# Attention kernel: the exponential of a pair of heads in two parts, with two sums

## The chip, the cores and the metric

The kernel runs on one core of a Trainium2 chip. The time is the device time of one execution in microseconds. The engines work side by side, each through its own list of instructions in order, and wait for each other through semaphores: TensorE (PE) does matrix products and transposes, VectorE (DVE) and ScalarE (ACT) work on tiles element by element, GpSimd (POOL) does slower side work, and SyncE (SP) issues the transfers.

## The reference

A block of a perceiver in float32: 32 batches of 64 queries, each against a context of 1601 keys of 256 features, in 16 heads of 16 features. After the cross-attention come a feed-forward part with cosines and a mixture of experts; the change touches only the attention. Its core is

```python
q = _split_heads(query @ Wq.T + bq)
k = _split_heads(key @ Wk.T + bk)
v = _split_heads(value @ Wv.T + bv)
score = jnp.einsum('bhqd,bhkd->bhqk', q, k) * SCALE
attn = jax.nn.softmax(score, axis=-1)
out = jnp.einsum('bhqk,bhkd->bhqd', attn, v)
out = out.transpose(0, 2, 1, 3).reshape(query.shape[0], query.shape[1], D)
return out @ Wp.T + bp
```

## The kernel before

The function `cross_attention` works through the 32 batches, and in each through 8 *pairs* of heads. One pair is a tile of 128 rows (two heads of 64 queries) by 1601 keys. The time in which TensorE takes one pair's scores is called a *slot* here, slots 0 to 7 in a batch. The running number of a pair is `g`, its number in the batch `p`.

What TensorE does in slot p, in its order (lines 643 to 695):

1. `scores(b, p)`, L587: four products into the four score banks `ps_s`. It waits until VectorE has read the scores of the pair before (`max_ready`).
2. Transposes 0 to 7 of the pair *before*, `turn(.., 0)` and `turn(.., 1)`, L598: each `turn` turns up to four blocks of 128 keys of `probs` into one of the two banks of `ps_t` (bank i % 2). They wait for the probabilities (`probs_ready`) and for their bank: `turn 0` for the copy that emptied bank 0 of the pair before that one (L595), `turn 1` for VectorE's copy of the tail from bank 1.
3. A step of the next batch's keys or values (L550 to L552). Slot p has the steps in `SLOT_STEPS` (L36), one to three.
4. Transposes 8 to 12, `turn(.., 2)` and `turn(.., 3)`: they wait until ScalarE has copied bank 0 and bank 1 of `turn 0` and `turn 1`.
5. In slots 0 and 4, after the transposes, the turned scale (L605) and `weigh` (L618), the product of four pairs' probabilities with the values. In the other slots, the rest of the steps.

ScalarE (lines 395 to 414) copies banks of transposes from PSUM to SBUF (L380, three copies of 512 columns for each pair) and takes the exponential of a whole pair in place (L386), with the row sum into `esum` by the accumulator output. That output is an instruction of its own, ACTIVATION_READ_ACCUMULATOR. In slots 0 and 4 the order is copy 0, copy 1, copy 2, exponential; in all other slots it is copy 0, copy 1, exponential, copy 2.

VectorE takes the minimum over a pair's negated scores and moves them to `probs` (L424, `take_scores`), which releases the exponential, adds the bias to the keys' steps and splits them in two (L442, L444), copies the values (L449) and the tail of the transposes (L456). Twice in a batch, in slots 0 and 4, `spread_scale` takes the reciprocals of four pairs' sums (L466) and spreads them over a tile (L468), ahead of `take_scores`.

The last batch has no steps of a next one. The order on every engine is written out by hand; no planner is at work.

Of the kernel before, what the change touches and what calls it, by code (L numbers as in the profile page):

```python
# [8 lines left out]
ALU = mybir.AluOpType  # L9
ACT = mybir.ActivationFunctionType  # L10
AX = mybir.AxisListType

P = 128
B, SQ, D = 32, 64, 256
SK = 1601
H, HD = 16, 16
NC = D // P
PAIRS = H // 2
# [19 lines left out]
HALF = PAIRS // NC  # L38
# [178 lines left out]
def cross_attention(nc, ctxT, x, q_scr, wk, bk, wv, bv, wp, rows, ident, x1_scr, x1_mv):  # L217
    with ExitStack() as ctx:
        sb = lambda n, s, d=F32: ctx.enter_context(nc.sbuf_tensor(n, s, d))
# [7 lines left out]
        probs = sb("a_probs", [P, 2, SKP])  # L227
# [9 lines left out]
        own = sb("a_own", [P, 2])  # L237
        tick = sb("a_tick", [P, 1])
        nmax = sb("a_nmax", [P, 2, PAIRS])
        esum, rinv = sb("a_esum", [P, 2, PAIRS]), sb("a_rinv", [P, HALF])  # L240
        scale = sb("a_sc", [P, HALF, 2, HD])
        scale_T, o_first = sb("a_sT", [P, 2 * SQ]), sb("a_os", [P, SQ])
        oT = sb("a_oT", [P, NC, P])
# [9 lines left out]
        s_filled, max_ready, probs_ready = sem("a_sf"), sem("a_mr"), sem("a_pr")  # L253
# [6 lines left out]
        first_banks = [ps_k[:]] + [ps_s[:, i, :] for i in range(QK)]  # L260
        bank_of = lambda s: ps_o if s % 2 else ps_k
        CONSTS = 5

        @block.sync
        def _(sp):
# [109 lines left out]
        @block.scalar  # L375
        def _(act):
            def copy_tiles(g, p, i):

                act.wait_ge(t_filled, TG * g + i + 1)
                nc.scalar.copy(pT[:, p % HALF, 4 * i:4 * i + 4, :], ps_t[:, i % 2, :].rearrange("p (t q) -> p t q", q=P)).then_inc(t_copied_act, 1)  # L380

            def exponentials(g, b, p):

                act.wait_ge(max_ready, g + 1)
                pr = probs[:, p % 2, 0:SK]
                nc.scalar.activation(pr, pr, ACT.Exp, bias=nmax[:, b, p:p + 1], scale=-1.0,  # L386
                                     accum_out=esum[:, b, p:p + 1]).then_inc(probs_ready, 1)

            act.wait_ge(w_loaded, 32)
            nc.scalar.copy(w_hi[:], w_raw).then_inc(w_hi_done, 1)  # L390
            act.wait_ge(first_loaded, 16)
            for k in range(NC):
                nc.scalar.copy(c_hi[:, 0, k, :], first_ctx[:, 0, k, :]).then_inc(ctx0_hi_done, 1)

            def body(it, first):
                for b in range(2):
                    n = 2 * it + b
                    for p in range(PAIRS):
                        g = PAIRS * n + p
                        prev = not first or b > 0 or p > 0  # L400
                        if prev:
                            copy_tiles(g - 1, (p - 1) % PAIRS, 0)
                            copy_tiles(g - 1, (p - 1) % PAIRS, 1)
                            if p % HALF == 0:
                                copy_tiles(g - 1, (p - 1) % PAIRS, 2)
                        exponentials(g, b, p)
                        if prev and p % HALF > 0:
                            copy_tiles(g - 1, (p - 1) % PAIRS, 2)

            for it in range(NT):  # L410
                body(it, it == 0)
            g = PAIRS * B - 1
            for i in range(3):
                copy_tiles(g, PAIRS - 1, i)

        @block.vector
        def _(dve):
# [44 lines left out]

            def spread_scale(w, pairs, b, h):

                dve.wait_ge(probs_ready, pairs)
                nc.vector.reciprocal(rinv[:], esum[:, b, HALF * h:HALF * (h + 1)]).then_inc(sum_inverse, 1)  # L466
                dve.wait_ge(sum_inverse, w + 1)
                nc.vector.tensor_tensor(scale[:], rinv[:].unsqueeze(2).unsqueeze(3).to_broadcast([P, HALF, 2, HD]),  # L468
                                        own[:].unsqueeze(1).unsqueeze(3).to_broadcast([P, HALF, 2, HD]), ALU.mult).then_inc(scale_ready, 1)

# [76 lines left out]
        def _(pe):  # L547
# [23 lines left out]
            def step_ahead(n, slot, s, it, first):  # L571

                if s == SLOT_STEPS[1][0]:
                    if not (isinstance(n, int) and n == 1):

                        pe.wait_ge(o_normed, 2 * n - 2)
                elif s == SLOT_STEPS[HALF + 1][0]:

                    pe.wait_ge(o_normed, 2 * n - 1)

                pe.wait_ge(kv_copied, STEPS * n + max(s - 1, 0))
                step(n, slot, s, bank_of(s))
# [7 lines left out]
            def turn(g, p, i, behind):  # L590

                if i >= 2:
                    pe.wait_ge(t_copied_act, 3 * g + i - 1)
                elif behind:
                    pe.wait_ge(t_copied_act if i == 0 else t_copied_dve, 3 * g if i == 0 else g)  # L595
                for t in range(4 * i, min(4 * i + 4, KT)):
                    r = rows_keys(t)
                    mm = nc.tensor.transpose(ps_t[0:r, i % 2, (t % 4) * P:(t % 4 + 1) * P],  # L598
                                             probs[:, p % 2, t * P:t * P + r], id_sb[:])
                mm.then_inc(t_filled, 1)  # L600
# [26 lines left out]

            pe.wait_ge(const_loaded, 16 * CONSTS)
            pe.wait_ge(w_split, 1)
# [8 lines left out]
            def body(it, first, last):  # L638
                for b in range(2):
                    n = 2 * it + b  # L640
                    ahead = not (last and b == 1)
                    pe.wait_ge(q_loaded, 96 * (n + 1))
                    for p in range(PAIRS):
                        g = PAIRS * n + p
                        prev = not first or b > 0 or p > 0
                        many = not first or b > 0 or p > 1
                        if p % HALF == 0:
                            for piece in stacked[p // HALF]:
                                pe.wait_ge(piece, COPIES * (n + 1))
                            if prev:  # L650

                                pe.wait_ge(max_ready, g)
                            scores(b, p)
                            if prev:
                                pe.wait_ge(probs_ready, g)
                                turn(g - 1, (p - 1) % PAIRS, 0, many)
                                turn(g - 1, (p - 1) % PAIRS, 1, many)
                            if ahead:
                                if p == 0:
                                    pe.wait_ge(ctx_split, NC * (n + 1))  # L660
                                step_ahead(n + 1, 1 - b, SLOT_STEPS[p][0], it, first)
                            if prev:
                                turn(g - 1, (p - 1) % PAIRS, 2, many)
                                turn(g - 1, (p - 1) % PAIRS, 3, many)
                                h, of = (1, 1 - b) if p == 0 else (0, b)
                                w = 2 * n - 1 if p == 0 else 2 * n
                                if b == 0 and p == HALF and not first:

                                    project_out(it - 1)
                                turn_scale(w)  # L670
                                if ahead and p == HALF:

                                    pe.wait_ge(kv_copied, STEPS * (n + 1) + SLOT_STEPS[HALF - 1][-1] + 1)
                                elif p == 0:
                                    pe.wait_ge(kv_copied, STEPS * (n + 1) - 1)
                                else:
                                    pe.wait_ge(o_normed, w)
                                weigh(g, of, h)
                        else:
                            steps = SLOT_STEPS[p] if ahead else ()  # L680

                            pe.wait_ge(max_ready, g)
                            scores(b, p)
                            pe.wait_ge(probs_ready, g)
                            turn(g - 1, p - 1, 0, many)
                            if b == 0 and p == HALF + 1 and not first:

                                pe.wait_ge(x1_ready, it)
                            turn(g - 1, p - 1, 1, many)
                            if steps:  # L690
                                step_ahead(n + 1, 1 - b, steps[0], it, first)
                            turn(g - 1, p - 1, 2, many)
                            turn(g - 1, p - 1, 3, many)
                            for s in steps[1:]:
                                step_ahead(n + 1, 1 - b, s, it, first)
# [1 line left out]
            for it in range(NT):  # L697
                body(it, it == 0, it == NT - 1)
            g = PAIRS * B - 1
            pe.wait_ge(probs_ready, g + 1)  # L700
            for i in range(TG):
                turn(g, PAIRS - 1, i, True)
            turn_scale(2 * B - 1)
# [905 lines left out]
```

## Time and profile before

| | us |
|---|---|
| median of 3 runs | 2150.76 (2149.16 to 2152.35) |
| profiled execution, its own time | 2150.42 |
| its span, first to last instruction | 2148.5 |
| TensorE busy | 1939.7 (90% of the span) |
| VectorE busy | 1524.4 (71%) |
| ScalarE busy | 1153.8 (54%) |
| GpSimd busy | 575.9 (27%) |
| L386, the exponential, 256 times | 418.9, mean 1.636 |
| L380, copies of transposes, 768 times | 421.6, mean 0.583 |
| L598, transposes, 3328 | 452.1 |

The attention stage takes from about 98 to 1495 us of the span. In a timeline each line has the start in us, the duration in us, the engine, the line of the kernel, the operation, the tiles written and read, and how many instructions are merged in it; in brackets stands the idle time before it and what ended that. PEld is TensorE's weight load, which runs beside its matmuls. Neighbouring instructions overlap in such rows, because the end of one is its last write, while the next may already have begun.

### The profile page before, as it was taken

To read this page: it belongs to the slowest core of one execution; us is meant where nothing else is said; L and a number is where in the kernel's file an instruction comes from. 1 tells how busy PE (TensorE), PEld (TensorE's weight loads), DVE (VectorE), ACT (ScalarE), POOL (GpSimd) and SP (SyncE) were. 2 spreads that over 40 slices of the span, in tenths; PEclk is the share of its full clock that TensorE was granted. 3 is DMA by queue.
4 is the path that set the end of the run, shared out by engine and by line. 5 is a ranking of instruction groups with operands and counts; after the bars stand their busy time and mean duration, and the time that the engine had idled before them with its cause. 6 is when DMAs were issued, how large, how long until landed. Compare 5 with 4: busy or idle time off the path is not lost. (4 is left out here: it accounts for less than half of the span.)

```text
span 2148.5 us, 47582 instructions
## 1 busy us (share of the span) xinstructions
PE 1939.7 (90%) x18832; PEld 1807.5 (84%) x18832; DVE 1524.4 (71%) x2830; ACT 1153.8 (54%) x1928; POOL 575.9 (27%) x543
## 2 busy tenths in 40 slices
PE   4699999999999999999999999996593499999988
PEld 2599999999999999999999999994373399999987
DVE  3577777777777777777777777774776167777745
ACT  3155656556555666565655655564752045555532
POOL 1223222332233222232233223301111603333342
PEclk8799999999999999999999999998696699999998
DMA  3666666666666666566666666652414445555522
GB/s 130 168 167 171 150 156 164 160 163 156 161 156 169 156 153 173 152 164 157 161 165 160 154 159 165 164 127 62 152 46 153 147 146 205 195 184 190 200 69 79
DMA packets 165281, 328.03 MB, mean 153 GB/s; under 512 B 58544, under 2 KB 96944, under 8 KB 161632
## 3 DMA queue, kind: packets, MB, share of 16 engines
q1 hardware_dynamic: 162016, 316.96, 53.4%
q0 software_dynamic: 3072, 8.39, 1.2%
q8 instruction: 134, 2.20, 0.5%
q14 instruction: 59, 0.48, 0.1%
HBM read 138.70 MB, written 28.44 MB: 78 GB/s over the span
## 5 line engine op out<-in xcount | busy, mean ns | idle before, releaser
L380 ACT COPY a_pT<-a_pst 128x512 f32<-128x512 f32 x768 | 421.6, 583 | 439.5 <-PE a_pst L598 439.3
L386 ACT ACTIVATE a_probs<-a_probs,a_nmax 128x1601 f32<-128x1601 f32 x256 | 418.9, 1636 | 146.2 <-DVE a_probs L424 146.2
L598 PE MATMUL a_pst<-a_id,a_probs 128*128 128x128 f32 (+1 forms) x3328 | 452.1, 274 | 28.8 <-ACT a_pT L380 26.2
L424 DVE TENSOR_SCALAR_CACHE_REDUCE a_probs<-a_pss 128x1608 f32<-128x1608 f32 x256 | 467.3, 1825 | 14.5 <-PE a_pss L587 12.4
L598 PEld LDWEIGHTS a_pst<-a_id,a_probs 128*128 128x128 f32 (+1 forms) x3328 | 381.6, 140 | 72.1 <-ACT a_probs L386 36.2
L348 POOL TENSOR_TENSOR a_tick<-a_tick 128x1 f32<-128x1 f32 x62 | 12.2, 197 | 979.1 <-DMA a_raw<-in_ctxT 964.1
L442 DVE TENSOR_SCALAR a_khi<-a_psk,a_bk 128x402 fp32r<-128x402 f32 x250 | 158.6, 634 | 144.7 <-PE a_psk L552 140.2
L353 POOL TENSOR_TENSOR a_clo<-a_raw,a_chi 128x402 fp32r<-128x402 f32 x240 | 246.6, 1060 | 4.8
L587 PE MATMUL a_pss<-a_kst,a_bd 96*128 96x402 f32 x1024 | 240.5, 357 | 6.8 <-DVE a_klo L444 6.8
L550 PE MATMUL a_pso<-a_whi,a_chi 128*128 128x256 f32 x806 | 241.3, 299 | 0.4 <-issue 0.4
L552 PE MATMUL a_pso<-a_whi,a_clo 128*128 128x256 f32 x806 | 227.0, 282 | 0.0
L551 PE MATMUL a_pso<-a_wlo,a_chi 128*128 128x256 f32 x806 | 226.5, 281 | 0.0
L550 PE MATMUL a_psk<-a_chi,a_whi 128*128 128x402 f32 x500 | 194.0, 388 | 22.3 <-DVE a_clo L504 22.3
L1458 PE MATMUL e_psg<-e_xh,e_guh 128*128 128x256 f32 x660 | 196.9, 298 | 18.1 <-DVE e_gul L1246 14.6
L587 PEld LDWEIGHTS a_pss<-a_kst,a_bd 96*128 96x128 f32 x1024 | 184.8, 190 | 20.5 <-issue 12.5
L618 PE MATMUL a_pso<-a_pT,a_v 128*32 128x128 f32 x6656 | 196.4, 274 | 2.1 <-DVE a_pT L456 1.9
L1460 PE MATMUL e_psg<-e_xh,e_gul 128*128 128x256 f32 x660 | 189.2, 287 | 3.5 <-issue 3.5
L1459 PE MATMUL e_psg<-e_xl,e_guh 128*128 128x256 f32 x660 | 188.8, 286 | 3.3 <-issue 3.3
L618 PEld LDWEIGHTS a_pso<-a_pT,a_v 128*32 128x32 f32 x6656 | 178.5, 110 | 15.2 <-issue 11.8
L552 PE MATMUL a_psk<-a_chi,a_wlo 128*128 128x402 f32 x500 | 174.3, 349 | 0.0
L551 PE MATMUL a_psk<-a_clo,a_whi 128*128 128x402 f32 x500 | 173.8, 348 | 0.0
L444 DVE SCALAR_TENSOR_TENSOR a_klo<-a_psk,a_bk,a_khi 128x402 fp32r<-128x402 f32 x250 | 159.0, 636 | 9.0
(225 smaller groups left out, 3572.0 us busy)
## 6 DMA issues: line engine op xcount, KB each, us to landing
a_kst<-a_khi SPq DMA_DIRECT2D x1024, 100.5 KB, 2.5
a_kst<-a_klo SPq DMA_DIRECT2D x512, 100.5 KB, 2.6
a_raw<-in_ctxT SPq DMA_DIRECT2D x60, 804.0 KB, 5.6
e_gur<-in_wgu SPq DMA_DIRECT2D x24, 1408.0 KB, 6.2
e_dr<-in_wd SPq DMA_DIRECT2D x24, 768.0 KB, 4.9
e_xb<-rows_scr SPq DMA_DIRECT2D x30, 256.0 KB
a_bd<-q_scr SPq DMA_DIRECT2D x192, 32.0 KB, 2.0
rows_scr<-f_zero SPq DMA_DIRECT2D x4, 1408.0 KB, 12.3
```

The source lines that it names most:

```text
L353: last = nc.gpsimd.tensor_tensor(out=c_lo[:, s, k, cols], in0=src[:, cols], in1=c_hi[:, s, k, cols].bitcast(F32), op=ALU.subtract)
L380: nc.scalar.copy(pT[:, p % HALF, 4 * i:4 * i + 4, :], ps_t[:, i % 2, :].rearrange("p (t q) -> p t q", q=P)).then_inc(t_copied_act, 1)
L386: nc.scalar.activation(pr, pr, ACT.Exp, bias=nmax[:, b, p:p + 1], scale=-1.0, accum_out=esum[:, b, p:p + 1]).then_inc(probs_ready, 1)
L424: nc.vector.tensor_scalar(probs[:, p % 2, :].rearrange("p (b k) -> p b k", b=QK), ps_s[:, :, 0:KQ], -1.0, None, ALU.mult, ALU.min, accum_o ...
L550: nc.tensor.matmul(out, a[0], b[0], start=start, stop=False)
L551: nc.tensor.matmul(out, a[0], b[1], start=False, stop=False)
L552: return nc.tensor.matmul(out, a[1], b[0], start=False, stop=stop)
L587: mm = nc.tensor.matmul(ps_s[:, q, 0:KQ], bd[:, b, p, :], k_st[:, p, q * KQ:(q + 1) * KQ], start=True, stop=True)
L598: mm = nc.tensor.transpose(ps_t[0:r, i % 2, (t % 4) * P:(t % 4 + 1) * P], probs[:, p % 2, t * P:t * P + r], id_sb[:])
L618: mm = nc.tensor.matmul(ps_o[32 * j:32 * j + 32, 0:P], v_sb[0:r, b, t, 32 * p:32 * p + 32], pT[0:r, j, t, :], start=(t == 0), stop=(t == K ...
L1458: nc.tensor.matmul(out, a[0], b[0], start=start, stop=False)
L1460: return nc.tensor.matmul(out, a[1], b[0], start=False, stop=stop)
```

## The change

The exponential becomes two, over the first 1024 keys and the last 577, each with a sum of its own and an increment of `probs_ready` of its own. So `probs_ready` counts two for each pair. The first two `turn`s wait for the first part, the last two for the second. `spread_scale` adds the two sums before the reciprocal. The order of the copies and of the exponentials on ScalarE is as it was.

```diff
-        esum, rinv = sb("a_esum", [P, 2, PAIRS]), sb("a_rinv", [P, HALF])
+        esum, rinv = sb("a_esum", [P, 2, 2, PAIRS]), sb("a_rinv", [P, HALF])
...
+        EXP_PARTS = (slice(0, 8 * P), slice(8 * P, SK))
...
-                pr = probs[:, p % 2, 0:SK]
-                nc.scalar.activation(pr, pr, ACT.Exp, bias=nmax[:, b, p:p + 1], scale=-1.0,
-                                     accum_out=esum[:, b, p:p + 1]).then_inc(probs_ready, 1)
+                for z, cols in enumerate(EXP_PARTS):
+                    pr = probs[:, p % 2, cols]
+                    nc.scalar.activation(pr, pr, ACT.Exp, bias=nmax[:, b, p:p + 1], scale=-1.0,
+                                         accum_out=esum[:, z, b, p:p + 1]).then_inc(probs_ready, 1)
...
-                dve.wait_ge(probs_ready, pairs)
-                nc.vector.reciprocal(rinv[:], esum[:, b, HALF * h:HALF * (h + 1)]).then_inc(sum_inverse, 1)
-                dve.wait_ge(sum_inverse, w + 1)
+                dve.wait_ge(probs_ready, 2 * pairs)
+                both = [esum[:, z, b, HALF * h:HALF * (h + 1)] for z in range(2)]
+                nc.vector.tensor_tensor(rinv[:], both[0], both[1], ALU.add).then_inc(sum_inverse, 1)
+                dve.wait_ge(sum_inverse, 2 * w + 1)
+                nc.vector.reciprocal(rinv[:], rinv[:]).then_inc(sum_inverse, 1)
+                dve.wait_ge(sum_inverse, 2 * w + 2)
...
                             if prev:
-                                pe.wait_ge(probs_ready, g)
+                                pe.wait_ge(probs_ready, 2 * g - 1)
                                 turn(g - 1, (p - 1) % PAIRS, 0, many)
                                 turn(g - 1, (p - 1) % PAIRS, 1, many)
...
                             if prev:
+                                pe.wait_ge(probs_ready, 2 * g)
                                 turn(g - 1, (p - 1) % PAIRS, 2, many)
                                 turn(g - 1, (p - 1) % PAIRS, 3, many)
...
-            pe.wait_ge(probs_ready, g + 1)
+            pe.wait_ge(probs_ready, 2 * (g + 1))
```

The slots other than 0 and 4 have the same two waits at the same places.

## Rows read from the trace of the kernel before

**Rows 1.** Busy time by stretch of the attention stage; columns in the first line

```profile
core 0: us, PE busy (x) PEld busy (x) DVE busy (x) ACT busy (x) POOL busy (x), PEclk, DMA share, GB/s
98.00:1447.00 1349.00, 1328.03 (x14566) 1263.36 (x14565) 1040.82 (x1880) 808.90 (x1235) 346.32 (x360) 1.00 0.64 159
1447.00:1495.00 48.00, 35.54 (x470) 28.39 (x468) 23.63 (x49) 28.99 (x46) 0.00 (x0) 0.96 0.15 35
```

**Rows 2.** Waits by releaser, 190 to 1447 us: total us, times, longest us

```profile
PEld a_pst L598 <- ACT a_probs L386: 23.6, 28, 0.9
PEld a_pst L598 <- issue: 20.1, 58, 0.4
PE a_pst L598 <- ACT a_pT L380: 14.8, 28, 0.5
```

**Rows 3.** Timeline of TensorE, slot 0: start, us, what; scores and transposes

```profile
836.64 0.90 PE L587 MATMUL a_pss<-a_kst,a_bd 96*128 96x402 f32 x4
838.08 1.07 PE L598 MATMUL a_pst<-a_id,a_probs 128*128 128x128 f32 x8 [0.54 <-ACT a_pT L380]
```

**Rows 4.** Timeline of ScalarE, slots 7 and 0

```profile
835.74 1.64 ACT L386 ACTIVATE a_probs<-a_probs,a_nmax 128x1601 f32<-128x1601 f32 x1 [0.62 <-DVE a_probs L424]
837.28 0.18 ACT L386 ACTIVATION_READ_ACCUMULATOR a_probs<-a_probs,a_nmax 128x1 f32 x1
837.37 0.56 ACT L380 COPY a_pT<-a_pst 128x512 f32<-128x512 f32 x1
841.21 1.64 ACT L386 ACTIVATE a_probs<-a_probs,a_nmax 128x1601 f32<-128x1601 f32 x1
```

**Rows 5.** Timeline of VectorE, slots 7 and 0

```profile
832.65 0.64 DVE L442 TENSOR_SCALAR a_khi<-a_psk,a_bk 128x402 fp32r<-128x402 f32 x1 [0.77 <-PE a_psk L552]
833.88 1.82 DVE L424 TENSOR_SCALAR_CACHE_REDUCE a_probs<-a_pss 128x1608 f32<-128x1608 f32 x1
838.07 0.17 DVE L466 RECIPROCAL a_rinv<-a_esum 128x4 f32<-128x4 f32 x1
840.23 0.08 DVE L424 DVE_READ_ACCUMULATOR a_probs<-a_pss 128x1 f32 x1
```

**Rows 6.** Timeline of TensorE, slots 2 and 3

```profile
804.62 0.90 PE L587 MATMUL a_pss<-a_kst,a_bd 96*128 96x402 f32 x4
805.36 1.04 PE L598 MATMUL a_pst<-a_id,a_probs 128*128 128x128 f32 x8
809.30 0.90 PE L587 MATMUL a_pss<-a_kst,a_bd 96*128 96x402 f32 x4
810.25 1.06 PE L598 MATMUL a_pst<-a_id,a_probs 128*128 128x128 f32 x8
```

**Rows 7.** Timeline of ScalarE, slots 2 and 3: the copies behind the exponentials

```profile
804.38 0.56 ACT L380 COPY a_pT<-a_pst 128x512 f32<-128x512 f32 x1
809.54 0.56 ACT L380 COPY a_pT<-a_pst 128x512 f32<-128x512 f32 x1
```

**Rows 8.** Timeline at the first pair of all: accumulator read, first weight loads

```profile
99.97 0.19 ACT L386 ACTIVATION_READ_ACCUMULATOR a_probs<-a_probs,a_nmax 128x1 f32 x1
100.21 0.86 PEld L598 LDWEIGHTS a_pst<-a_id,a_probs 128*128 128x128 f32 x8 [0.58 <-ACT a_probs L386]
```

**Rows 9.** Timeline of ScalarE in the later feed-forward stage: neighbours with a bias tile

```profile
1513.05 0.68 ACT L976 ACTIVATE f_c<-f_t,f_hp 128x480 f32<-128x480 f32 x1
1513.63 0.61 ACT L972 ACTIVATE f_t<-f_t 128x512 f32<-128x512 f32 x1
1516.49 1.08 ACT L976 ACTIVATE f_c<-f_t,f_hp 128x960 f32<-128x960 f32 x1
1517.48 4.02 ACT L960 ACTIVATE f_u<-f_x,f_sft,f_scl 128x256 f32<-128x256 f32 x8
```

**Rows 10.** Timeline of the last batch: one exponential, the next transposes

```profile
1478.99 1.64 ACT L386 ACTIVATE a_probs<-a_probs,a_nmax 128x1601 f32<-128x1601 f32 x1
1481.34 1.06 PE L598 MATMUL a_pst<-a_id,a_probs 128*128 128x128 f32 x8 [1.12 <-ACT a_pT L380]
```

More of the change, by code:

```diff
@@ L683, in body @@
                             scores(b, p)
-                            pe.wait_ge(probs_ready, g)
+                            pe.wait_ge(probs_ready, 2 * g - 1)
                             turn(g - 1, p - 1, 0, many)
@@ L691, in body @@
                                 step_ahead(n + 1, 1 - b, steps[0], it, first)
+                            pe.wait_ge(probs_ready, 2 * g)
                             turn(g - 1, p - 1, 2, many)
```

## The prediction, made before the changed kernel ran

> **What bounds the kernel now.** The page's busy table and the stretch table come first. In the attention stage, from 98 to 1447 us, TensorE is busy 1328 of 1349 us at full granted clock, while ScalarE is busy 809 us [rows 1]. So TensorE sets the pace, at most some 21 us of its gaps are there to be won, and everything that delays TensorE lengthens the kernel.
>
> Second, the waits. From 190 to 1447 us there are 29 batches. The first transpose of a slot (a slot is one pair of heads: its scores, the transposes of the pair before, a step of the next batch's keys or values) waits 28 times for about 0.53 us and 58 times for 0.35 us in the weight load [rows 2]. That is one long wait and two short ones for each batch. One row names the exponential (L386) as the releaser, another the copy (L380), and the change is worth something only if the first name is the right one.
>
> Third, the timeline, to settle this. In slot 0 the scores start at 836.64 and the transposes at 838.08 [rows 3]. On ScalarE the exponential starts at 835.74, its accumulator read ends at 837.28 + 0.18 = 837.46, and the copy of transposes 8 to 11 (bank 0) of the pair before ends at 837.37 + 0.56 = 837.93 [rows 4]. TensorE starts 0.62 us after the exponential's sum and 0.15 us after the copy. For the very first pair, where no copy stands between, the weight load starts at 100.21 and the sum is done at 99.97 + 0.19 = 100.16, only 0.05 us before [rows 8]. So in slot 0 the wait is for the copy, that is for PSUM bank 0 to be free (line 595), and not for the probabilities. ScalarE issues this copy behind the exponential in every slot but 0 and 4.
>
> The short waits are the same. In slot 3 the scores start at 809.30 and the transposes at 810.25, 0.95 us later, against 0.74 us where nothing waits (804.62 and 805.36) [rows 6]. The copy ends at 809.54 + 0.56 = 810.10, again 0.15 us ahead [rows 7]. The stall is 0.95 - 0.74 = 0.21 us in slots 3 and 7, and 1.44 - 0.74 = 0.70 us in slot 0. In slot 2 the copy ends at 804.94, so it would allow a start at 805.09, 0.27 us before TensorE comes to it; slot 6 is alike. In slots 1 and 5 ScalarE has made the copy before the exponential, and nothing waits.
>
> **The change part by part.** *The exponential in two.* ScalarE now issues ACTIVATE, accumulator read, ACTIVATE, accumulator read, and only then the copy that frees bank 0. The elements are the same 1601, so what is added, called X, is one fixed part of an ACTIVATE and one accumulator read. Start to start, ACTIVATEs with a bias tile take 0.58 us for 480 columns and 0.99 for 960 [rows 9]: 0.854 ns a column and 0.17 us fixed. This line gives 1.54 us for 1601 columns, and the row has 837.28 - 835.74 = 1.54 [rows 4]. For 1024 and 577 columns it gives 1.045 + 0.663 = 1.708 us, 0.17 more. The accumulator read takes 0.09 us from its start to the copy's (837.28 to 837.37). I take X = 0.17 + 0.09 = 0.26 us. No row shows an ACTIVATE behind an accumulator read, so I bound X. From below it is 0.09 us, if the second fixed part vanished; it cannot be below that, since no work is taken away. From above it is 0.47 us, if nothing overlapped: the 0.28 us that separate the 0.68 us of a 480-column ACTIVATE from 480 x 0.835 ns (slope of the durations 0.68 and 1.08), and the whole 0.19 us of the read. The 0.26 is nearest to the rows, for they show exactly such neighbours overlapping.
>
> The Trainium skill prices this in "ScalarE: Activation LUTs", What ACT_TABLE_LOAD costs: 280 ns plus 0.833 ns a column with a bias tile, and 93 ns of overlap back to back. That agrees with the rows' slope and makes a split cost 0.187 us, but it has no price for the accumulator read; by it alone the sum below would be 12.7 us instead of 17.7.
>
> *Where X lands.* Scores of a slot stand before its transposes, and the minimum on VectorE that releases the exponential hangs on the key step that ends the slot before: L442 waits for that step, and L444 and L424 follow it without a gap [rows 5]. So in slot 2 the copy is X late against slot 1's end, and slot 3's transposes start X later. Slot 2's own delay, X less the 0.27 us of slack, is nothing at 0.26 and would be swallowed in slot 3 anyway. Slots 4 and 5 pass the delay on unchanged, as their transposes find the bank free long before. Slot 6 has 0.27 us of slack and hides X = 0.26; slot 7 adds X. The exponential of slot 7 starts after slot 6's key step, so it has only slot 6's delay; its copy is X later than that, and slot 0 comes out with (X of slots 2 and 3) + X + max(0, X - 0.27). At 0.26 slot 7's X and slot 0's X are one and the same delay. The sum is 2X + max(0, X - 0.27) = 0.52 us a batch.
>
> The 31 batches that prepare a next one give 31 x 0.52 = 16.1 us. The last batch has no steps to fill TensorE. There it waits 1.1 us for the copy in every slot but 1 and 5, and ScalarE's exponential starts right behind its copies [rows 10], so each of the six exponentials with a copy behind it costs its X: 1.6 us. Together 17.7 us. The very first pair gains up to 1.72 - 1.045 - 0.19 = 0.49 us, the one place where the transposes wait for probabilities; slot 2's bank wait takes it back, and I count it at nothing.
>
> *The waits on TensorE.* The first eight transposes wait for part one and the rest for part two. In slots 2, 3, 4, 6, 7 and 0 the bank is free only after a copy that ScalarE issues behind both parts; in slots 1 and 5 both parts are long done. So the earlier release is worth nothing. The second wait is met for the same reason when TensorE comes to it behind a step of over 1 us. Queued behind it are the last five transposes and then the next scores.
>
> *The sums on VectorE.* One tensor_tensor of four columns and one more wait come in twice a batch. The nearest row is the reciprocal of four columns, 0.17 us [rows 5]; I take 0.2 us, between 0.1 and 0.4. In slot 0 the minimum behind it is ready at 840.23 + 0.08 = 840.31, and the exponential starts only at 841.21, behind a copy [rows 4, 5]. That 0.90 us hides it; if the cover were gone, it would cost 64 x 0.2 = 13 us. The reciprocal at 838.07 comes after both parts even with X added (837.46 + 0.26). No DMA and no other queue is moved.
>
> **The rivals.** *Faster: the probabilities are the gate.* If the transposes of slots 3, 7 and 0 waited for the exponential, as one row of the waits names it, the first part would be ready 0.49 us sooner. That would give back 0.21 + 0.21 + 0.49 = 0.91 us a batch, 28 us in all: 2122 us. For it: the row of 23.6 us [rows 2]. Against it: the 0.15 us behind the copy, three slots alike, beside 0.62 us behind the sum. It decides if transposes start within 0.1 us of a sum.
>
> The Trainium skill has a rule for this side, in "Perfetto Trace Analysis", Optimizing Scalar/DVE Operations: where ScalarE isn't saturated but causes bubbles elsewhere, breaking up its instructions may let work finish sooner. Both its conditions hold here; what the trace adds is that the bubble hangs on the instruction behind the one that is broken up.
>
> *Hardly slower: the second ACTIVATE's fixed part vanishes.* X is 0.09 us: 31 x 0.18 + 6 x 0.09 = 6 us, 2156.5 us; if still less landed, no change. Against it: the line through rows 9 also fits 1601 columns.
>
> *Much slower: the next ACTIVATE waits until the accumulator is read.* X is 0.47: slots 2 and 6 have no slack left, 31 x (3 x 0.47 - 0.27) + 6 x 0.47 = 38 us, 2188.5 us. For it: both parts use the same accumulator, which a copy doesn't. Against it: no row shows such a pause.
>
> **How the numbers follow.** The profiled execution took 2150.42 us (span 2148.5), 0.3 us below the median of the runs. 2150.4 + 17.7 = 2168.1 us. I give the forecast 0.62, hardly slower or nothing 0.14, much slower 0.18, faster 0.06. The range 2155 to 2182 reaches from X = 0.07 to X = 0.40. A change below 0.2% (4.3 us) can't be told from none; half of the second case lies there: slower 0.87, same 0.07, faster 0.06.
>
> **What would show it.** Right: between the start of the first ACTIVATE and that of the copy 1.89 instead of 1.63 us; transposes still starting 0.15 us after the copy in slots 3, 7 and 0; slot 0's offset from scores to transposes still over 1.4 us; a batch 0.5 us longer; nothing changed after 1500 us but a shift. Wrong: transposes that start before the copy of the pair before has ended, a copy less than 0.1 us later, or a stall in slots 1, 4 or 5.

## The result, and the profile after

The changed kernel takes 2176.11 us (median of 4, 2174.72 to 2177.96), the kernel before 2150.79 us: ratio 1.0118, 95% interval 1.0101 to 1.0136. The change makes it 25 us slower. The forecast was 2168, range 2155 to 2182.

In the page, ScalarE has 72 us more to do and TensorE 7:

```profile
PE 1946.6 (90%) x18832; PEld 1807.0 (83%) x18832; DVE 1541.7 (71%) x2894; ACT 1226.1 (56%) x2440; POOL 574.0 (26%) x543
```

The groups of ScalarE by form (line, operation, tiles, shapes, count, busy us, mean ns, idle before):

```profile
L388 ACT ACTIVATE a_probs<-a_probs,a_nmax 128x1024 f32<-128x1024 f32 x256 | 294.9, 1152 | 130.9 <-DVE a_probs L426 130.4
L388 ACT ACTIVATE a_probs<-a_probs,a_nmax 128x577 f32<-128x577 f32 x256 | 195.8, 765 | 0.0
L388 ACT ACTIVATION_READ_ACCUMULATOR a_probs<-a_probs,a_nmax 128x1 f32 x512 | 95.8, 187 | 0.0
```

ScalarE's timeline in slots 7 and 0 of one batch, which answers to [rows 4] (L388 was L386, L381 was L380):

```profile
797.09 1.15 ACT L388 ACTIVATE a_probs<-a_probs,a_nmax 128x1024 f32<-128x1024 f32 x1 [0.36 <-DVE a_probs L426]
798.14 0.19 ACT L388 ACTIVATION_READ_ACCUMULATOR a_probs<-a_probs,a_nmax 128x1 f32 x1
798.23 0.77 ACT L388 ACTIVATE a_probs<-a_probs,a_nmax 128x577 f32<-128x577 f32 x1
798.90 0.19 ACT L388 ACTIVATION_READ_ACCUMULATOR a_probs<-a_probs,a_nmax 128x1 f32 x1
798.99 0.56 ACT L381 COPY a_pT<-a_pst 128x512 f32<-128x512 f32 x1
```

The copy starts 798.99 - 797.09 = 1.90 us after the exponential, where [rows 4] have 1.63: X is 0.27 us here, 0.28 in its neighbours, against 0.26 in the forecast. The first part's sum is done at 798.33 and the copy at 799.55. TensorE's timeline of the same two slots (L592 the scores, L603 the transposes) answers to [rows 3]:

```profile
793.79 0.89 PE L592 MATMUL a_pss<-a_kst,a_bd 96*128 96x402 f32 x4
794.98 1.06 PE L603 MATMUL a_pst<-a_id,a_probs 128*128 128x128 f32 x8 [0.30 <-ACT a_pT L381]
798.25 0.91 PE L592 MATMUL a_pss<-a_kst,a_bd 96*128 96x402 f32 x4
799.70 1.07 PE L603 MATMUL a_pst<-a_id,a_probs 128*128 128x128 f32 x8 [0.54 <-ACT a_pT L381]
```

The transposes start at 799.70, again 0.15 us after the copy and 1.37 us after the part that they are said to wait for. Slot 7 has grown from 0.93 or 0.95 us between scores and transposes to 1.19; slot 0 stays at 1.45. The waits from 190 to 1447 us, for [rows 2]:

```profile
PEld a_pst L603 <- ACT a_probs L388: 58.1, 85, 0.9
PE a_pst L603 <- ACT a_pT L381: 32.1, 85, 0.6
PEld a_pst L603 <- issue: 12.6, 57, 2.2
PE a_pst L603 <- issue: 3.3, 2, 1.9
```

TensorE waits for the copy 85 times instead of 28. Taking the medians of the distances between the starts of the scores over batches 2 to 29, a batch takes 44.14 us where it took 43.57: 0.57 us more. Over those 28 batches that is 16.0 us, but the stretch is 1244.4 - 1221.0 = 23.4 us longer. The other 7.4 us are a few slots that are much longer than their like. The worst one starts at 961.43:

```profile
961.43 1.01 PE L592 MATMUL a_pss<-a_kst,a_bd 96*128 96x402 f32 x4
964.37 1.94 PE L603 MATMUL a_pst<-a_id,a_probs 128*128 128x128 f32 x8 [1.93 <-issue]
```

TensorE is idle for 1.93 us with nothing in the profile that it waits for ("issue"). The granted clock by stretch (the third number from the end) shows what follows:

```profile
961.00:962.40 1.40, 1.40 (x24) 0.89 (x13) 0.65 (x3) 0.00 (x0) 0.00 (x0) 1.00 1.07 283
962.40:964.30 1.90, 0.03 (x1) 0.00 (x0) 1.83 (x2) 0.00 (x0) 0.85 (x2) 0.98 0.86 208
964.30:966.00 1.70, 1.64 (x9) 1.67 (x9) 0.01 (x2) 0.51 (x1) 1.62 (x2) 0.50 0.81 206
966.00:968.20 2.20, 2.20 (x14) 2.20 (x13) 0.00 (x0) 1.93 (x5) 2.20 (x4) 0.62 0.27 65
968.20:970.00 1.80, 1.80 (x14) 1.80 (x13) 0.88 (x2) 1.22 (x3) 1.05 (x2) 1.00 0.00 0
```

From the end of the stop the clock is at half, 1.2 GHz, for 3.4 us (0.50 in the third stretch, 0.62 in the fourth), and the slot is 3.7 us longer than its like. Six long slots, all in slots 4, 5 and 0 of batches 4, 9, 14, 19 and 29, cost 8.6 us; the kernel before has two, 1.1 us together. Five of the six have a stop on "issue" of over 0.4 us, but only the one shown is followed by half clock. In the other slots the granted clock stays full, and the slot is longer by little more than its stop.

### The profile page after: what moved, and what is told of

Same layout as the page of the kernel before. It is cut to its first block and busy times, and to the rows that moved or that the text cites. A ratio compares the mean times of both kernels' runs of the same rounds, so it can differ in the third digit from the quotient of the medians.

```text
span 2172.9 us, 48413 instructions
## 1 busy us (share of the span) xinstructions
PE 1946.6 (90%) x18832; PEld 1807.0 (83%) x18832; DVE 1541.7 (71%) x2894; ACT 1226.1 (56%) x2440; POOL 574.0 (26%) x543
## 5 line engine op out<-in xcount | busy, mean ns | idle before, releaser
L381 ACT COPY a_pT<-a_pst 128x512 f32<-128x512 f32 x768 | 421.2, 583 | 406.4 <-PE a_pst L603 406.4
L388 ACT ACTIVATE a_probs<-a_probs,a_nmax 128x1024 f32<-128x1024 f32 (+1 forms) x512 | 489.6, 958 | 130.9 <-DVE a_probs L426 130.4
L603 PE MATMUL a_pst<-a_id,a_probs 128*128 128x128 f32 (+1 forms) x3328 | 456.7, 276 | 48.7 <-ACT a_pT L381 45.3
L603 PEld LDWEIGHTS a_pst<-a_id,a_probs 128*128 128x128 f32 (+1 forms) x3328 | 379.1, 141 | 98.7 <-ACT a_probs L388 74.2
L592 PE MATMUL a_pss<-a_kst,a_bd 96*128 96x402 f32 x1024 | 240.8, 357 | 9.2 <-DVE a_klo L446 6.8
L592 PEld LDWEIGHTS a_pss<-a_kst,a_bd 96*128 96x128 f32 x1024 | 185.1, 191 | 23.3 <-issue 15.3
L1404 ACT ACTIVATE e_sg<-e_psg 128x256 f32<-128x256 f32 x180 | 68.5, 380 | 178.5 <-PE e_psg L1467 115.4
```

Of the source, the lines that this page charges most:

```text
L592: mm = nc.tensor.matmul(ps_s[:, q, 0:KQ], bd[:, b, p, :], k_st[:, p, q * KQ:(q + 1) * KQ], start=True, stop=True)
```

## The experiments

The comparisons ran on two other chips, where the kernel before takes 2096 us instead of 2151. Each kernel is therefore compared with the kernel before on its own chip, and the absolute times in the first expectations are to be read as differences. Theory 1 is the forecast's: bank 0 is the gate, and X makes it later. Theory 2, formed on the trace above, is that the stops come with TensorE's second wait.

**one_release.** The early release alone undone.

```diff
-                            pe.wait_ge(probs_ready, 2 * g - 1)
+                            pe.wait_ge(probs_ready, 2 * g)
...
```

> The changed kernel, but the first eight transposes wait for the second part too, as the last five do: the early release is gone, the two ACTIVATEs stay. Theory 1 (bank): the transposes wait for the copy that frees bank 0, which ScalarE issues behind both parts, so the release is worth nothing: the changed kernel's 2176 us within 2 us. Rival (the early release pays part of the split back): slower, by up to 0.9 us a batch, some 28 us, 2204 us.

Measured 2125.58 against 2096.86 us before: ratio 1.0145 (1.0126 to 1.0163), 28.7 us. The number expected, 2176 us, is void, as the chip is another; the comparison is not. The changed kernel has 1.0140 (1.0119 to 1.0160) on its later chip, and the median batch is 44.14 us in both. The early release is worth nothing in this order of ScalarE.

**no_second_sum.** The second ACTIVATE has no accumulator output, so the row sums leave out the last 577 keys.

```diff
-                    nc.scalar.activation(pr, pr, ACT.Exp, bias=nmax[:, b, p:p + 1], scale=-1.0,
-                                         accum_out=esum[:, z, b, p:p + 1]).then_inc(probs_ready, 1)
+                    acc = dict(accum_out=esum[:, 0, b, p:p + 1]) if z == 0 else {}
+                    nc.scalar.activation(pr, pr, ACT.Exp, bias=nmax[:, b, p:p + 1], scale=-1.0, **acc).then_inc(probs_ready, 1)
...
+            nc.vector.memset(esum[:, 1], 0.0)
```

> The changed kernel without the accumulator output of the second part (the row sum leaves out the last 577 keys; the second half of the sums is set to zero once). One accumulator read less, 0.09 us: X falls from the measured 0.28 to 0.19 us. Theory 1: 31 batches x (2 x 0.09 + 0.01) + 6 x 0.09 = 6 us less, 2170 us. Rival (the price of the change lies on TensorE's waits or on VectorE, not in ScalarE's path before the copy): 2176 us, unchanged.

Measured 2116.41, ratio 1.0093 (1.0076 to 1.0111): 9.2 us less than one_release on the same chip, where 6 were expected. X is 0.19 us in its trace, as expected. The price lies in ScalarE's path before the copy. Median batches are 43.91 against 44.14 us, 7 us over 31; the rest is within the spread.

**three_parts.** X doubled. The waits count three for each pair, and the row sums leave out the last part.

```diff
-        EXP_PARTS = (slice(0, 8 * P), slice(8 * P, SK))
+        EXP_PARTS = (slice(0, 8 * P), slice(8 * P, 10 * P), slice(10 * P, SK))
...
```

> The exponential in three parts of 1024, 256 and 321 keys (the row sum leaves out the last 321). X doubles to 0.56 us. Theory 1: 31 x (3 x 0.56 - 0.27) + 6 x 0.56 = 47 us over before where the split in two has 19 by the same formula; the stops of issue of the changed kernel (some 6 us) come on top: 2198 to 2204 us, and the wait now shows in slots 2 and 6 as well, 0.29 us each. Rival (X costs nothing more once it is above the slack, because another engine sets the pace): under 2190 us.

Measured 2153.24, ratio 1.0267 (1.0249 to 1.0286): 56.4 us over before, where 47 to 53 with the stops were expected, and 27.7 over one_release; 47 - 19 = 28 were expected. X is 0.56 us in its trace, and the median batch is 44.97 us, 0.83 more than with two parts. Slots 2 and 6 now wait as well, 0.28 us (their offset goes from 0.75 to 1.03), as forecast. The law 2X + max(0, X - 0.27) holds at both values.

**all_but_split.** The exponential in one again, TensorE's second waits and VectorE's extra sum left in.

```diff
-                for z, cols in enumerate(EXP_PARTS):
-                    pr = probs[:, p % 2, cols]
...
+                pr = probs[:, p % 2, 0:SK]
+                nc.scalar.activation(pr, pr, ACT.Exp, bias=nmax[:, b, p:p + 1], scale=-1.0,
+                                     accum_out=esum[:, 0, b, p:p + 1]).then_inc(probs_ready, 2)
...
+            nc.vector.memset(esum[:, 1], 0.0)
```

> The changed kernel with the exponential in one instruction again, which raises the count by two; the second waits of TensorE and the extra sum of VectorE stay (the second half of the sums is zero). Theory 1: nothing of this is on the path, 2151 us, as before. Theory 2 (TensorE's own waits make its instruction stream longer or slower, and cause the 6 us of stops of issue in the changed kernel): 2155 to 2158 us.

Measured 2110.49, ratio 1.0057 (1.0035 to 1.0079): 13.6 us slower than before, though ScalarE does no more. Theory 1 alone is refuted on this point; theory 2 has the direction, but its 4 to 7 us were half of what came. In its trace the long slots sum to 12 us, and TensorE's idle time on "issue" alone, from 190 to 1400 us, is:

```profile
PE a_pss L592 <- issue: 5.0, 4, 1.8
PE a_pst L603 <- issue: 1.9, 1, 1.9
PE a_pso L623 <- issue: 0.2, 1, 0.2
```

Besides, in every slot but 0 its exponentials start 0.10 us after the minimum (807.98 and 808.08) where the kernel before has 0.04, and slots 3 and 7 are 0.06 us longer, 3 us in all. Why is left open; the split kernels have 0.04 again.

**waits_only.** The kernel before with nothing but the second waits.

```diff
+                            pe.wait_ge(probs_ready, g)
                             turn(g - 1, p - 1, 2, many)
...
```

> The kernel before, with only a second wait for the same pair's exponential put ahead of transposes 8 to 12, one in each slot; nothing of ScalarE or VectorE is touched. Theory 2 (the longer instruction stream of TensorE puts its fetches at places where its issue stops): 7 to 12 us slower than before, with stops of issue in slots 4, 5 and 0 of every fifth batch. Rival (the cost of the kernel with all but the split came from VectorE's extra sum): no change.

Measured 2098.71 against 2095.57, ratio 1.0021 (1.0005 to 1.0037): 3.1 us, where 7 to 12 were expected; the 12 runs spread from 2090.9 to 2105.7. In the trace the stops are there, in slots 5 and 0 of batches 14, 19, 24 and 29, 5.9 us in all, and every median slot is as before. The waits suffice to bring stops, but how much these cost differs from kernel to kernel. In none of the four stops here, of up to 1.68 us, does half clock follow, and all_but_split has it twice.

**changed_again and changed_no_second_wait.** The changed kernel once more, and without the second wait. ScalarE copies bank 0 of a pair only after both parts of its exponential, so `turn 2`, which waits for that copy, needs no other.

```diff
-                            pe.wait_ge(probs_ready, 2 * g)
                             turn(g - 1, p - 1, 2, many)
...
```

> The changed kernel itself, on the chip of these comparisons. Both theories: 25 to 29 us slower than before (25.3 us where it was first timed; 28.7 us for its twin with one release).

> The changed kernel without TensorE's second wait: ScalarE makes copy 0 of a pair only after both parts of its exponential, so the wait for that copy covers it. Theory 1 and 2: ScalarE's X stays, the stops go: 19 us slower than before, 6 to 9 us faster than the changed kernel of this call. Rival (the stops have nothing to do with these waits): the same as the changed kernel.

Measured on one chip: 2125.54, ratio 1.0140 (1.0119 to 1.0160), 30.0 us slower than before; without the wait 2116.60, ratio 1.0098 (1.0077 to 1.0118), 21.0 us slower. The wait costs 9 us, and what is left is near the 19 of theory 1. The long slots sum to 9.8 us with it and to 0.3 without. TensorE's waits in the changed kernel, 190 to 1400 us:

```profile
PE a_pst L603 <- ACT a_pT L381: 30.8, 82, 0.6
PE a_pss L592 <- issue: 3.9, 4, 2.1
PE a_pst L603 <- issue: 1.7, 1, 1.7
```

and without the second wait, where no row of PE on issue is left:

```profile
PE a_pst L603 <- ACT a_pT L381: 30.8, 81, 0.7
```

The wait for the copy is the same 30.8 us in both. The profile of waits_only counts 47,837 instructions where the kernel before has 47,582, which is 255 more, one for each slot after the first. The queue that carries instructions (packets, MB, share) has one packet of 16 KB more in every kernel with the second waits, first the changed kernel, then the one without them:

```profile
q8 instruction: 135, 2.21, 0.5%
```

```profile
q8 instruction: 134, 2.20, 0.4%
```

So the waits are further instructions in TensorE's stream.

The records of this queue also show what ends a stop. In the traces of all kernels, from 190 to 1447 us, TensorE has 34 stops on issue of over 0.4 us, all of them in kernels with the second waits. Before each of them a packet of this queue starts 20 to 23 us behind the one before it, where the usual distance is some 12 us, and in 33 of the 34 TensorE goes on 1.2 to 1.7 us after that packet has ended. The stop at 962.43 is an example: no packet of the queue starts from 941.7 to 961.6 us, then comes this one in the view of 961.6 to 962.8. It starts at 961.69 and ends at 962.73, and TensorE goes on at 964.37.

```profile
q8 instruction: 1, 0.02, 5.4%
```

The packet itself takes 1.04 us, no longer than others; it is its start that is late. This points to TensorE waiting for its instructions; no run moves a packet alone to prove it. Why a packet starts late is not shown. A context's transfer, issued at 957.03, is under way then, but such a transfer is issued in slot 4 of 30 batches, and few of them have a stop. A long distance isn't enough either: the kernel before has a packet 21.7 us behind its predecessor, and TensorE stops for only 0.36 us, at 869.05.

**copy_first_single.** The kernel before with ScalarE's order changed.

```diff
                             copy_tiles(g - 1, (p - 1) % PAIRS, 1)
-                            if p % HALF == 0:
-                                copy_tiles(g - 1, (p - 1) % PAIRS, 2)
+                            copy_tiles(g - 1, (p - 1) % PAIRS, 2)
                         exponentials(g, b, p)
-                        if prev and p % HALF > 0:
-                            copy_tiles(g - 1, (p - 1) % PAIRS, 2)
```

> The kernel before, with only ScalarE's order changed: in every slot copy 2 comes before the exponential, which stays one instruction. Now the bank is free early and the transposes of the next slot wait for the whole exponential. From the start of transposes 8 to 12 it takes 0.63 us to the copy, 0.49 to the exponential, 1.72 to its sum and 0.05 to TensorE, 2.89 us where TensorE needs 2.38: a stall of 0.5 us in five slots instead of 1.12 us in three. Theory 1 (bank): +1.4 us a batch, 43 us slower than before. Rival (the order of ScalarE is of no weight): no change.

Measured 2143.35 against 2096.25, ratio 1.0234 (1.0214 to 1.0255): 47.1 us slower, where 43 were expected. The waits from 190 to 1400 us:

```profile
PE a_pst L595 <- ACT a_probs L386: 45.9, 134, 0.4
```

Now the releaser is the exponential, five times a batch, and the copy no longer appears.

**copy_first_split and copy_first_one_release.** The same order in the changed kernel, and there without the early release.

> The changed kernel with copy 2 before both parts in every slot. The wait is then for the probabilities and the first part is 0.47 us sooner than the whole: 2.42 us against the 2.38 that TensorE needs. Theory 1: the stalls of slots 3, 7 and 0 go, 0.92 us a batch, 28 us faster than before, less some 7 to 11 us for the stops of issue that come with TensorE's second waits: 17 to 28 us faster. Rival (the split costs ScalarE too much in any place): slower than before.

> As the kernel with the copy before both parts, but all transposes wait for the second part. This shows what the early release is worth once the probabilities are the gate: 3.17 us against 2.38, a stall of 0.79 us in five slots. Theory 1: 2.8 us a batch, some 85 us slower than before and over 110 us slower than its partner with the early release. Rival (early release worth nothing here either): within 5 us of its partner.

Measured 2070.72, ratio 0.9885 (0.9867 to 0.9904), 25.5 us faster than before; without the early release 2197.32, ratio 1.0487 (1.0468 to 1.0505), 101 us slower. In this order the early release is worth 126.6 us, in the order of the changed kernel nothing. Expected were 17 to 28 us faster, some 85 slower and over 110 between the two. TensorE and ScalarE in slots 7 and 0 of the faster one (L589 scores, L600 transposes):

```profile
821.27 0.90 PE L589 MATMUL a_pss<-a_kst,a_bd 96*128 96x402 f32 x4
822.03 1.09 PE L600 MATMUL a_pst<-a_id,a_probs 128*128 128x128 f32 x8
```

```profile
820.25 0.59 ACT L381 COPY a_pT<-a_pst 128x512 f32<-128x512 f32 x1 [0.51 <-PE a_pst L600]
820.74 1.15 ACT L388 ACTIVATE a_probs<-a_probs,a_nmax 128x1024 f32<-128x1024 f32 x1
821.79 0.19 ACT L388 ACTIVATION_READ_ACCUMULATOR a_probs<-a_probs,a_nmax 128x1 f32 x1
821.88 0.76 ACT L388 ACTIVATE a_probs<-a_probs,a_nmax 128x577 f32<-128x577 f32 x1
```

The first part's sum ends at 821.98 and the transposes start at 822.03, 0.76 us after the scores: slot 0's 0.70 us of stall are gone. A median batch takes 42.83 us, 0.74 less than before. It has the second waits, too, yet it has no row of PE on issue and its long slots sum to 0.6 us. So the waits alone don't decide on the stops. From 190 to 1447 us its instruction packets are never more than 17.6 us apart.

**copy_between.** Copy 2 between the two parts.

```diff
-                        exponentials(g, b, p)
+                        exponential(g, b, p, 0)
                         if prev and p % HALF > 0:
                             copy_tiles(g - 1, (p - 1) % PAIRS, 2)
+                        exponential(g, b, p, 1)
```

> The changed kernel with copy 2 between the two parts. The copy ends 0.48 us sooner than in the kernel before, and the first part is done before it. Theory 1: slots 3 and 7 lose their 0.21 us, slot 0 is left with some 0.2 to 0.4 of 0.70 us: 0.69 us a batch, 21 us faster than before, less 7 to 11 us of stops of issue. Rival: slower than before, by X on ScalarE.

Measured 2073.61, ratio 0.9894 (0.9876 to 0.9913), 22.6 us faster. Expected were 21 us less 7 to 11 for stops; its long slots sum to only 2.5 us. The median batch is 42.85 us; slots 3 and 7 start at 0.75 us after their scores, slot 0 at 1.17 instead of 1.44. The waits, 190 to 1400 us:

```profile
PE a_pst L604 <- ACT a_pT L381: 7.4, 28, 0.3
```

**copy_first_no_second_wait.**

> The fastest kernel so far (copy before both parts, early release), without TensorE's second wait. Its trace had only 0.6 us of stops of issue. Theory 1: within 3 us of its partner, 24 to 30 us faster than before. Theory 2 as a rule for every kernel with the waits would make it 7 us faster than its partner, 33 us faster than before.

Measured 2073.54, ratio 0.9888 (0.9868 to 0.9907), 22.0 us faster, a little less than the 24 to 30 expected, and the same as its partner within the intervals. Where there were no stops, leaving the wait out gains nothing.

## Why the prediction was right, and where it was short

*The gate.* Right. The transposes start 0.15 us after the copy in the changed kernel too; one_release shows that the release is worth nothing, and with the copy out of the way the same release is worth 126.6 us. The rival "the probabilities are the gate" is out.

*X.* Forecast 0.26 us, measured 0.28. The accumulator read added its 0.09 us, and the two ACTIVATEs together take 1152 + 765 = 1917 ns where one took 1636. "Much slower", a pause behind the accumulator read, is out: the second ACTIVATE starts 0.09 us after the start of the read. "Hardly slower" is out as well.

*The law.* Forecast 0.52 us a batch, measured 0.57; it gives 0.57 with X = 0.28. For three parts (X = 0.56) it gives 1.41 and the median batch shows 1.40; without the second sum (X = 0.19) it gives 0.38, and 0.34 is measured.

*VectorE.* The extra sum is no wait of TensorE in any trace, and its usual size was right: 0.2 us in the forecast, 0.15 in the median. The cover was read in slot 0 only, where the sum always takes 0.15 us:

```profile
L469 DVE TENSOR_TENSOR a_rinv<-a_esum x64: 151/154/982, 114.2 to 1507.1; 128x4 f32<-128x4 f32 x64
```

In slot 4 it takes up to 0.98 us, well over the 0.4 of the forecast, and the cover there was never 0.90 us but 0.04 to 0.80 in the kernel before. In more than half of the batches the exponential of slot 4 now starts right behind the minimum. What keeps this off the path is something else: the first part of that exponential is done at least 2.0 us before slot 5's transposes start, and these still start 0.85 us after their scores. Here the forecast was right for a reason that it didn't give.

*The second waits of TensorE.* This is the term that failed: costed at nothing, because what they wait for is long there. As a wait they do cost nothing. As instructions they come with stops of issue, one of which is followed by 3.4 us of half clock in the changed kernel's first trace. That is 8.6 - 1.1 = 7.5 us between the two profiles of the first chip, 9 us between the changed kernel and its twin without them. The forecast's 17.7 us, 1.6 more for the larger X and 7.5 for the stops make 26.8; the profiled executions are 2174.72 - 2150.42 = 24.3 us apart. Outside of this, batch 2 begins 4.6 us sooner in the changed trace and the part after the last scores is 3.1 us longer; neither is explained. That the total still lies in the range is in part luck: the range was made for X from 0.07 to 0.40 us and holds no term for the stops.

## What to carry to other kernels

Before an instruction is split so that its first part can release someone early, look at what else the waiting engine needs: if a buffer is freed by work that is queued behind the split instruction, the split makes that later. Reorder the queue first; here each edit alone costs time, 30 us and 47 us, and together they gain 25. An added wait that is always met is still an instruction; where an existing wait implies it, leave it out.

## What the runs showed of the hardware

- TensorE can stop with no data missing. In 33 of the 34 stops it goes on 1.2 to 1.7 us after the end of a packet of the instruction queue that starts 20 to 23 us behind the one before.
- After some stops the granted clock is at half for 3.4 us. In the attention this followed five of the 34 stops: one of 1.68 us (no_second_sum) and four of 1.85 to 2.12 us (the changed kernel's two traces and all_but_split). It didn't follow two of 2.12 us (no_second_sum and three_parts), nor any other. All the three stops of 2.12 us lie in slot 5 of batch 9: with half clock the slot is 3.9 us longer than its like, without it 2.3 us.
- VectorE's sum of four columns takes 0.15 us alone and up to 0.98 us beside GpSimd. Each of the 24 that took 0.2 us or more ends within 0.03 us after the end of a GpSimd instruction that was under way when it started, here one that ends at 823.09:

```profile
821.03 2.06 POOL L354 TENSOR_TENSOR a_clo<-a_raw,a_chi 128x402 fp32r<-128x402 f32 x2
822.33 0.79 DVE L469 TENSOR_TENSOR a_rinv<-a_esum 128x4 f32<-128x4 f32 x1
```

- The kernel before takes 2151 us on one chip and 2096 on two others. Its median batch in the attention is 43.57 us on the first, and the same in waits_only on another. The difference lies behind the attention: from the last scores to the end of the span it is 669.3 us on the first chip and 616.2 in waits_only. Part of it is in the experts' stage: in the stretch from 1640 to 1700 us TensorE is busy 15.5 us on the first chip, and 34.3 us on the other (waits_only, where the attention ends 1.2 us later):

```profile
1640.00:1700.00 60.00, 15.47 (x90) 14.15 (x90) 20.84 (x61) 7.50 (x12) 33.04 (x32) 0.59 0.64 228
1700.00:1760.00 60.00, 49.38 (x368) 46.69 (x369) 28.57 (x53) 21.08 (x49) 10.48 (x9) 0.88 0.29 101
```

```profile
1640.00:1700.00 60.00, 34.32 (x244) 32.53 (x245) 31.72 (x92) 14.20 (x31) 31.99 (x30) 0.73 0.63 224
1700.00:1760.00 60.00, 58.98 (x463) 56.19 (x463) 46.64 (x65) 32.36 (x68) 28.00 (x18) 1.00 0.58 211
```

The changed kernel's first trace has the same slow part (672.4 us from the last scores to the end, where changed_again has 619.3), so it doesn't bear on the comparison. What causes it is not shown.
